# A short convolution moved from VectorE to TensorE: four diagonal tap matrices per channel block, accumulated in PSUM

## The chip, the cores and the metric

The kernel runs on one core of one Trainium2 chip. The metric is the device time of one execution in microseconds (us). In a profile PE is TensorE's matmul side and PEld its weight loads, DVE is VectorE, ACT is ScalarE, POOL is GpSimd, and SP is SyncE, which here only issues DMAs.

## What is computed

One block of a network with adaptive layer norm, on 16 sequences of 512 steps and 256 channels in float32: a modulated layer norm, a bidirectional Mamba (two directions, 512 inner channels, 64 states, a causal convolution of 4 taps per channel), a second norm, and a gated network with 1024 hidden units. The part that matters is, for each direction:

```python
xz = x @ W_in.T
xp, z = jnp.split(xz, 2, axis=-1)
xc = conv_general_dilated(xp.transpose(0, 2, 1), conv_w[:, None, :], window_strides=(1,),
                          padding=[(K - 1, 0)], feature_group_count=E)      # K = 4 taps, E = 512 channels
xc = _silu(xc.transpose(0, 2, 1) + conv_b)
x_dbl = xc @ W_xp.T                       # dt_lo, B, C
dt = softplus(dt_lo @ W_dt.T + dt_b)
h = exp(dt * A) * h + (dt * xt) * B       # a scan over 512 steps, for 512 channels x 64 states
y = sum_n(h * C)
```

## The kernel before, in words

**The loop.** The program handles one sequence per *body*: a preparation body ("pre"), then "first", 14 times "mid" (a hardware loop), "last" and "tail". A body with scans has 128 *units*, 64 for each direction. A unit is 4 states of 128 channels: a tile `state` of 128 partitions by 2048 elements, handled in two halves of 1024.

**The scan pipeline.** For each unit ACT makes the decays (L985, four activations), the input of the scan `driven` is made in PSUM, DVE scans it (L1196, one `TENSOR_TENSOR_SCAN` per half), POOL multiplies the result by C (L1226, one per half), and PE sums over states into `y_ps` (L824, `accumulate`). In even units DVE makes `driven` itself (L1185), from rows that PE spreads into `b_ps` (L800). In odd units ACT (L998) and POOL (L1234) make `v_sb`, and PE transposes it into `driven` (L810, `drive`). Two halves of `driven` exist, so that PE's transposes for half h of an odd unit wait for the scan of half h of the even unit before.

**The side work.** Everything else is put between the units by tables (`side_steps`), as (unit, part, name, count): in a unit each engine first does its share of the scan pipeline and then its side steps. Part "early" and "late" are the previous sequence's output and hidden network (PE bank `q_ps`), "p1" is the second direction of this sequence (steps from unit `P1_AT` = 12), "next" the first direction of the next sequence (from `NEXT_AT` = 80); p1, next and the eight transposes `UT0` to `UT7` of the scan's input share the bank `p_ps`. Each engine runs its instructions in the order written, and each step in a bank waits (`bank_free`) until the step before it in the same bank has been read out.

**The convolution.** In p1 and next, for each of four channel blocks m, three units apart: PE makes the projection X (two matmuls of 128x512, L681) into `p_ps`; ACT copies it to `u_sb`, the inner part of `u_pad` whose first three columns are zero (L889), and writes tap 0 plus the bias into `xc` (L892); DVE adds taps 1, 2 and 3 with three `scalar_tensor_tensor` (L1156, steps `conv{m}0` and `conv{m}1`). Then ACT applies silu to `xc` (L896), and PE makes B, C and dt from it. In a mid body the blocks of p1 start in units 14, 17, 20 and 23 and those of next in 82, 85, 88 and 91.

**Other work in the same units.** In p1's units 15 to 22 DVE has the residual mix and a layer norm of part early. In next's units PE has the hidden network's first layer (`F`, four matmuls of 128x256 in each of units 77 to 84) and second layer (`H`, four in each of units 89 to 104); DVE multiplies the gate (`glu`, L1139, units 86 and 87) once ACT's silu of unit 85 is done (L957).

**Queues.** SP issues all DMAs in order: in each unit `c_rep` (256 KB, L504, which waits for POOL's reading of two units before), and between them `ud_rep`, weights, stores. `dt_sb` (128 partitions by 8 KB) holds dt, is written in the steps D (L918) and stored to DRAM by `store_ud`; between this store and the next stage's D it is not used, except that C is staged in its first block.

## Time and profile before

| | |
|---|---|
| median of 3 runs | 14339.97 us (14336.53 to 14356.86) |
| the profiled execution | 14347.66 us |
| its span in the profile | 14345.8 us |
| first scan to the end | from 146.8 us on |
| TensorE clock granted, mean | 0.81 |

A row of the costliest groups reads: line, engine, operation, tile written <- tiles read, count | busy us in all, mean ns of one | idle us of the engine just before them, and who ended most of it. A row of a timeline reads: start us, duration us, engine, line, what, count of instructions merged, and in brackets the idle time before it. PE's fp32 matmuls stand in the trace as two records each, so that two matmuls of 128x512 read "x4".

### The profile page before, as it was taken

How to read it: one execution, taken by the hardware profiler on the slowest of the kernel's cores; microseconds unless marked ns; L12 is line 12 of the kernel's file. 1: busy time of each engine (PE TensorE's matmuls, PEld its weight loads, DVE VectorE, ACT ScalarE, POOL GpSimd, SP SyncE). 2: the span in 40 equal slices, each digit the busy share in tenths (PEclk: the TensorE clock that was granted, in tenths of full speed). 3: DMA queues.
4: the chain of work that ended last, by engine and by line, in shares of the span. 5: the costliest groups of instructions: out<-in, count | busy, mean ns of one | idle time of the engine just before them, and what ended most of it. 6: DMA issues, size and time to landing. Idle time of an engine off the chain costs nothing.

```text
span 14345.8 us, 177084 instructions
## 1 busy us (share of the span) xinstructions
PE 10529.0 (73%) x50188; PEld 6035.3 (42%) x50188; DVE 13278.1 (93%) x8254; ACT 10969.1 (76%) x23324; POOL 10908.2 (76%) x5124
## 2 busy tenths in 40 slices
PE   5567767777676777767777777776777767777776
PEld 2234434444343443434434344443444434344345
DVE  6999999999999999999999999999999999999992
ACT  5777777788777887778777777777777877787782
POOL 4887777787777777778777777777777777777781
PEclk7778878788787887878888788887878878788798
DMA  2223323333232332323322233232333323233232
GB/s 72 80 82 98 103 89 108 99 104 104 90 107 95 107 105 95 106 91 109 107 95 96 94 109 105 97 102 91 107 98 105 104 88 107 95 108 103 94 110 87
DMA packets 596164, 1414.30 MB, mean 99 GB/s; under 512 B 63488, under 2 KB 104592, under 8 KB 594976
## 3 DMA queue, kind: packets, MB, share of 16 engines
q1 hardware_dynamic: 595104, 1402.00, 29.9%
q8 instruction: 441, 7.23, 0.2%
q14 instruction: 619, 5.07, 0.1%
HBM read 1313.57 MB, written 88.18 MB: 98 GB/s over the span
## 4 chain that ended last, share of the span: by engine, by line
issue 26%; PE 26%; DVE 24%; ACT 20%; POOL 3%; DVEq 1%; DMA 0%; ACTq 0%; POOLq 0%; SPq 0%
DVE state L1196 13%; PE driven L810 7%; ACT state L985 7%; ACT v_sb L998 6%; PE q_ps L765 6%; DVE driven L1185 3%; POOL state L1226 3%; PE y_ps L824 3%; PE p_ps L681 2%; PE q_ps L752 2%; DVE xc L1156 2%; PE b_ps L800 2%; PE q_ps L775 1%; ACT L985 1%; PE p_ps L688 1%
## 5 line engine op out<-in xcount | busy, mean ns | idle before, releaser
L1226 POOL TENSOR_TENSOR state<-state,c_rep 128x1024 f32<-128x1024 f32 x4096 | 9764.5, 2406 | 3006.0 <-DVE state L1196 3005.4
L1196 DVE TENSOR_TENSOR_SCAN state<-state,driven 128x1024 f32<-128x1024 f32 x4096 | 9106.1, 2270 | 444.8 <-PE driven L810 274.1
L998 ACT ACTIVATE v_sb<-u_t,b_t 128x128 f32<-128x128 f32 x12288 | 3992.7, 505 | 2226.7 <-PE driven L810 2224.8
L985 ACT ACTIVATE state<-ud_rep,cols_sb 128x512 f32<-128x512 f32 x8192 | 5185.8, 710 | 2.4 <-PE y_ps L824 0.2
L824 PE MATMUL y_ps<-state,consts_sb 128*32 128x512 f32 x16384 | 2666.9, 729 | 2292.1 <-POOL state L1226 2289.1
L810 PE MATMUL driven<-consts_sb,v_sb 128*128 128x128 f32 x16384 | 2957.9, 344 | 1122.8 <-DVE state L1196 1113.4
L810 PEld LDWEIGHTS driven<-consts_sb,v_sb 128*128 128x128 f32 x16384 | 2432.5, 179 | 2576.9 <-DVE state L1196 2134.0
L1185 DVE TENSOR_TENSOR driven<-ud_rep,b_ps 128x1024 f32<-128x1024 f32 x2048 | 2390.2, 1213 | 16.9 <-DMA ud_rep<-ud_rows 16.9
L765 PE MATMUL q_ps<-hid,wq_sb 128*128 128x256 f32 x8192 | 2231.1, 420 | 130.0 <-ACT hid L963 83.4
L765 PEld LDWEIGHTS q_ps<-hid,wq_sb 128*128 128x128 f32 x8192 | 1596.9, 205 | 926.1 <-issue 671.7
L824 PEld LDWEIGHTS y_ps<-state,consts_sb 128*32 128x32 f32 x16384 | 347.5, 117 | 3418.0 <-POOL state L1226 3027.9
L1234 POOL TENSOR_TENSOR v_sb<-u_t,b_t 128x512 f32<-128x512 f32 x1024 | 1220.1, 1191 | 140.0 <-ACT u_t L913 140.0
L681 PE MATMUL p_ps<-x_t,wp_sb 128*128 128x512 f32 x1024 | 580.0, 695 | 20.7 <-ACT sz L936 14.5
L800 PE MATMUL b_ps<-b_parts,onehot 32*128 32x512 f32 x1024 | 587.1, 573 | 0.0
L752 PE MATMUL q_ps<-xn_q,wq_sb 128*128 128x256 f32 x2048 | 542.3, 410 | 44.3 <-ACT hid L953 39.9
L963 ACT ACTIVATE hid<-q_ps,cols_sb 128x256 f32<-128x256 f32 x512 | 239.0, 467 | 436.6 <-PE q_ps L765 436.2
L1156 DVE SCALAR_TENSOR_TENSOR xc<-u_pad,cols_sb,xc 128x512 f32<-128x512 f32 x384 | 510.5, 1329 | 51.6 <-ACT xc L892 40.5
L752 PEld LDWEIGHTS q_ps<-xn_q,wq_sb 128*128 128x128 f32 x2048 | 388.6, 200 | 243.0 <-issue 143.9
L775 PE MATMUL q_ps<-wq_sb,hid 128*128 128x256 f32 x1024 | 308.5, 454 | 37.1 <-ACT hid L968 30.1
L681 PEld LDWEIGHTS p_ps<-x_t,wp_sb 128*128 128x128 f32 x1024 | 208.8, 214 | 264.9 <-issue 212.9
L953 ACT ACTIVATE hid<-q_ps,cols_sb 128x256 f32<-128x256 f32 x512 | 212.6, 468 | 138.0 <-PE q_ps L752 137.7
L800 PEld LDWEIGHTS b_ps<-b_parts,onehot 32*128 32x128 f32 x1024 | 214.5, 209 | 227.0 <-issue 227.0
(113 smaller groups left out, 5202.5 us busy)
## 6 DMA issues: line engine op xcount, KB each, us to landing
c_rep<-bc_rows SPq DMA_DIRECT2D x2048, 256.0 KB, 3.0
ud_rep<-ud_rows SPq DMA_DIRECT2D x512, 512.0 KB, 3.9
wq_sb<-in_h SPq DMA_DIRECT2D x512, 512.0 KB, 3.8
wq_sb<-in_f SPq DMA_DIRECT2D x128, 512.0 KB, 4.4
wp_sb<-in_win SPq DMA_DIRECT2D x64, 512.0 KB, 3.8
ud_rows<-u_pad SPq DMA_DIRECT2D x128, 256.0 KB, 3.3
ud_rows<-dt_sb SPq DMA_DIRECT2D x128, 256.0 KB, 3.4
u_nat<-ud_rows SPq DMA_DIRECT2D x128, 256.0 KB, 3.1
```

The lines of the kernel that those rows point to most:

```text
L681: mm = pe.matmul(p_ps[:], wp_sb[:, m, k, :], x_t[:, k, :], start=(k == 0), stop=(k == DC - 1))
L752: mm = pe.matmul(q_ps[:, which * TH:(which + 1) * TH], w[:, m % 2, which, k, :], n_t[:, k, i * TH:(i + 1) * TH], start=(k == 0), stop=(k = ...
L765: mm = pe.matmul(q_ps[:, 0:TH], w[:, k, :], src[:, k, :], start=(k == 0), stop=(k == HC - 1))
L800: pe.matmul(b_ps[:], onehot[k, g % quarter, :], b_parts[d][k, :], start=True, stop=True).then_inc(b_spread, 1)
L810: mm = pe.transpose(driven[:, q % DRIVE_RING, j % 2, tt * P:(tt + 1) * P], v_sb[:, unit // 2 % V_RING, tt, j].rearrange("p e n -> p (e n)" ...
L824: mm = pe.matmul(y_ps[EG * j:EG * (j + 1), :], over_nn, state[:, k % STATE_RING, j, :], start=(g == 0), stop=(g == NG - 1))
L985: ins = act.activation(state[:, unit % STATE_RING, j, :], ud_rep[:, nth % 2, j, 1, :], ACT.Exp, scale=a_neg[:, d, c, j, g:g + 1])
L998: ins = act.activation(v_sb[:, unit // 2 % V_RING, tt, :, :, n].rearrange("p j e -> p (j e)"), u_t[:, nth % 2, tt, :], ACT.Identity, scale ...
L1185: dve.tensor_tensor(driven[:, h], u_rows(unit)[:, 2 * h:2 * h + 2], b_ps[:].unsqueeze(1).to_broadcast([P, 2, T]), ALU.mult).then_inc(dve_d ...
L1196: dve.tensor_tensor_scan(flat, flat, driven[:, q % DRIVE_RING].rearrange("p j t -> p (j t)"), 0.0, ALU.mult, ALU.add).then_inc(scanned, 1)
L1226: pool.tensor_tensor(part, part, c_rep[:, unit % ROW_RING, :].unsqueeze(1).to_broadcast([P, 2, T]), ALU.mult).then_inc(was_read, 1)
L1234: pool.tensor_tensor(v_sb[:, unit // 2 % V_RING, TT - 1].rearrange("p j e n -> p (j e) n"), u_t[:, nth % 2, TT - 1, :].unsqueeze(2).to_bro ...
```

## The change

The four taps of a channel block become four matmuls whose stationary matrix is the diagonal matrix of one tap (128x128) and whose moving operand is `u_pad` shifted by the tap's number of columns, all accumulated in `p_ps` (step `K{m}`, two matmuls in each of the two units after X). ACT then writes `xc` from `p_ps` with the bias in one activation; the activation for tap 0 and DVE's three instructions per block go. The matrices are made once at the start by ACT (32 activations of 128x128 into `ud_rep`), stored to a DRAM tensor of 2 MB, and loaded, 1 MB for each direction, into `dt_sb` (`load_conv`), in unit 8 for p1 and 76 for next. The transposes `UT2`, `UT6` and `UT7` move from units 25, 89 and 106 to 26, 78 and 97.

```diff
-UT_AT = (120, 10, 25, 41, 57, 73, 89, 106)
+UT_AT = (120, 10, 26, 41, 57, 73, 78, 97)
...
-        act.append((x, part, f"X{m}", 2))
-        dve += [(x + 1 + i, part, f"conv{m}{i}", 1 + i) for i in range(2)]
+        act.append((x, part, f"X{m}", 1))
+        pe += [(x + 1 + i, part, f"K{m}", i) for i in range(2)]
+        act.append((x + 2, part, f"K{m}", 1))
...
+        conv_dram = nc.dram_tensor("conv_taps", (2, P, EC * TAPS * P), F32, kind="Internal").ap()
...
+        conv_w = dt_sb[:].rearrange("p c t -> p (c t)").rearrange("p (c k n) -> p c k n", c=EC, k=TAPS)
...
+            sp.wait_ge(setup_act, 4)
+            sp.dma_start(conv_dram.rearrange("d p n -> p d n"),
+                         conv_made.rearrange("p d c k n -> p d (c k n)")).then_inc(conv_stored, 16)
             sp.wait_ge(mod_stored, 16)
+            sp.wait_ge(conv_stored, 16)
...
+            def load_conv(at, part):
+
+                if at.kind != "pre":
+                    wait(ud_out.sem, ud_out.before(at) if part == "p1" else ud_out.done(at, "p1", "ud"))
+                d = 1 if part == "p1" else 0
+                sp.dma_start(dt_sb[:].rearrange("p c t -> p (c t)"), conv_dram[d]).then_inc(conv_in.sem, 16)
...
+                    if unit == P1_AT - 4 and at.has("p1"):
+                        load_conv(at, "p1")
+                    if unit == NEXT_AT - 4 and at.has("next"):
+                        load_conv(at, "next")
...
+                elif name[0] == "K":
+                    m = int(name[1])
+                    if quarter == 0:
+                        pe.wait_ge(act_side.sem, act_side.done(at, part, f"X{m}"))
+                        if m == 0:
+                            pe.wait_ge(conv_in.sem, conv_in.done(at, part, "conv"))
+                    for k in range(2 * quarter, 2 * quarter + 2):
+                        mm = pe.matmul(p_ps[:], conv_w[:, m, k, :], u_pad[:, m, k:k + T], start=(k == 0), stop=(k == TAPS - 1))
...
+            for d in range(2):
+                for c in range(EC):
+                    for k in range(TAPS):
+                        ins = act.activation(conv_made[:, d, c, k, :], ident, ACT.Identity, scale=taps[:, d, c, k:k + 1])
+            ins.then_inc(setup_act, 1)
...
-                        act.wait_ge(done, act_side.done(at, part, name, 0))
-                        act.activation(xc_sb[d][:, m, :], u_pad[:, m, 0:T], ACT.Identity, bias=conv_b[:, d, m:m + 1],
-                                       scale=taps[:, d, m, 0:1]).then_inc(done, 1)
+                    elif kind == "K":
+                        after_pe(pe_p)
+                        act.activation(xc_sb[d][:, m, :], p_ps[:], ACT.Identity, bias=conv_b[:, d, m:m + 1]).then_inc(done, 1)
                     elif name == "xc":
-                        act.wait_ge(dve_side.sem, dve_side.done(at, part, "conv31"))
+                        act.wait_ge(done, act_side.done(at, part, "K3"))
...
-                    if name.startswith("conv"):
-                        m, last = int(name[4]), int(name[5])
-                        if not last:
-                            dve.wait_ge(act_side.sem, act_side.done(at, part, f"X{m}"))
-                        dst = xc_sb[d][:, m, :]
-                        for i in ((2, 3) if last else (1,)):
-                            emit(dve.scalar_tensor_tensor(dst, u_pad[:, m, i:i + T], taps[:, d, m, i:i + 1], dst,
-                                                          ALU.mult, ALU.add), i < TAPS - 1)
```

**Order on PE, units 91 to 93 of a mid body (part next).** Before, from the transposes for unit 93 on; `q_ps` is the hidden network, `y_ps` the sum over states:

```order
L810 MATMUL driven<-consts_sb,v_sb 128x128 x16
L797 REGISTER_ALU
L800 MATMUL b_ps<-b_parts,onehot 128x512
L765 MATMUL q_ps<-hid,wq_sb 128x256 x4
L822 REGISTER_ALU
L824 MATMUL y_ps<-state,consts_sb 32x512 x4
L650 REGISTER_ALU
L762 REGISTER_ALU
L765 MATMUL q_ps<-hid,wq_sb 128x256 x4
```

The same place with the change, where the four matmuls of block 3's taps stand in units 92 and 93:

```order
L840 MATMUL driven<-consts_sb,v_sb 128x128 x16
L827 REGISTER_ALU
L830 MATMUL b_ps<-b_parts,onehot 128x512
L795 MATMUL q_ps<-hid,wq_sb 128x256 x4
L672 REGISTER_ALU
L711 MATMUL p_ps<-u_pad,dt_sb 128x512 x2
L852 REGISTER_ALU
L854 MATMUL y_ps<-state,consts_sb 32x512 x4
L672 REGISTER_ALU
L792 REGISTER_ALU
L795 MATMUL q_ps<-hid,wq_sb 128x256 x4
L711 MATMUL p_ps<-u_pad,dt_sb 128x512 x2
```

Each of the two units now has a second side step on PE, between the transposes and the next sums.

**Order on ACT, units 84 and 85 of a mid body.** Before, from the first part of `v_sb` in unit 84 to the silu (L957) of the hidden network:

```order
L998 ACTIVATE v_sb<-u_t,b_t 128x128 x4
L866 REGISTER_ALU
L953 ACTIVATE hid<-q_ps,cols_sb 128x256 x2
L998 ACTIVATE v_sb<-u_t,b_t 128x128 x8
L985 ACTIVATE state<-ud_rep,cols_sb 128x512 x4
L956 REGISTER_ALU
L957 ACT_TABLE_LOAD
L957 ACTIVATE hid<-hid 128x2048
```

With the change:

```order
L1033 ACTIVATE v_sb<-u_t,b_t 128x128 x4
L901 REGISTER_ALU
L988 ACTIVATE hid<-q_ps,cols_sb 128x256 x2
L901 REGISTER_ALU
L928 ACTIVATE xc<-p_ps,cols_sb 128x512
L1033 ACTIVATE v_sb<-u_t,b_t 128x128 x8
L1020 ACTIVATE state<-ud_rep,cols_sb 128x512 x4
L991 REGISTER_ALU
L992 ACT_TABLE_LOAD
L992 ACTIVATE hid<-hid 128x2048
```

The read-out of block 0's taps now stands in unit 84 ahead of the decays and the silu, and waits for PE's second pair of tap matmuls.

## Rows read from the trace of the kernel before

**Rows 1.** The profile's page, part 1: busy time of each engine over the span.
```profile
PE 10529.0 (73%) x50188; PEld 6035.3 (42%) x50188; DVE 13278.1 (93%) x8254; ACT 10969.1 (76%) x23324; POOL 10908.2 (76%) x5124
```
**Rows 2.** The page, part 5: costliest groups.
```profile
L1196 DVE TENSOR_TENSOR_SCAN state<-state,driven 128x1024 f32<-128x1024 f32 x4096 | 9106.1, 2270 | 444.8 <-PE driven L810 274.1
...
L998 ACT ACTIVATE v_sb<-u_t,b_t 128x128 f32<-128x128 f32 x12288 | 3992.7, 505 | 2226.7 <-PE driven L810 2224.8
...
L681 PE MATMUL p_ps<-x_t,wp_sb 128*128 128x512 f32 x1024 | 580.0, 695 | 20.7 <-ACT sz L936 14.5
...
L1156 DVE SCALAR_TENSOR_TENSOR xc<-u_pad,cols_sb,xc 128x512 f32<-128x512 f32 x384 | 510.5, 1329 | 51.6 <-ACT xc L892 40.5
```
**Rows 3.** Timeline of DVE, units 78 to 80, where it has no side step.
```profile
3260.49 8.81 DVE L1196 TENSOR_TENSOR_SCAN state<-state,driven 128x1024 f32<-128x1024 f32 x4
3269.22 2.33 DVE L1185 TENSOR_TENSOR driven<-ud_rep,b_ps 128x1024 f32<-128x1024 f32 x2
3271.46 4.46 DVE L1196 TENSOR_TENSOR_SCAN state<-state,driven 128x1024 f32<-128x1024 f32 x2
```
**Rows 4.** Windows of one body's two convolution stretches, line L1156 alone: DVE busy, clock, DMA.
```profile
2816.00:2916.00 100.00, 15.60 (x12) 0.67 0.18 56
3283.00:3373.00 90.00, 16.42 (x12) 0.82 0.28 95
```
**Rows 5.** The view of line L1156: durations in ns, min/median/max.
```profile
L1156 DVE SCALAR_TENSOR_TENSOR xc<-u_pad,cols_sb,xc x384: 736/962/2808, 61.0 to 13441.3; 128x512 f32<-128x512 f32 x192
```
**Rows 6.** Waits of DVE in that body (2722 to 3599): total, times, longest, in us.
```profile
DVE state L1196 <- PE driven L810: 17.4, 13, 4.2
...
DVE xc L1156 <- ACT xc L892: 1.5, 2, 1.2
DVE state L1196 <- DVE xc L1156: 1.2, 4, 0.6
```
**Rows 7.** Timeline of PE, units 100 to 102: two side steps in each unit.
```profile
3416.47 1.97 PE L810 MATMUL driven<-consts_sb,v_sb 128*128 128x128 f32 x16
...
3418.80 1.99 PE L765 MATMUL q_ps<-hid,wq_sb 128*128 128x256 f32 x8
3420.63 1.89 PE L697 MATMUL p_ps<-sz,xc 128*128 128x64 f32 x16
...
3428.10 1.97 PE L810 MATMUL driven<-consts_sb,v_sb 128*128 128x128 f32 x16
```
**Rows 8.** Timeline of PE, units 88 to 91: a wait, and two projections X.
```profile
3333.09 1.97 PE L810 MATMUL driven<-consts_sb,v_sb 128*128 128x128 f32 x8 [2.80 <-DVE state L1196]
...
3337.89 3.65 PE L681 MATMUL p_ps<-x_t,wp_sb 128*128 128x512 f32 x4
...
3354.81 1.88 PE L681 MATMUL p_ps<-x_t,wp_sb 128*128 128x512 f32 x4
```
**Rows 9.** Timelines of ACT, units 84 and 85, and of DVE at the gate, unit 86.
```profile
3303.28 1.42 ACT L998 ACTIVATE v_sb<-u_t,b_t 128x128 f32<-128x128 f32 x4 [0.62 <-PE driven L810]
...
3314.47 1.91 ACT L957 ACTIVATE hid<-hid 128x2048 f32<-128x2048 f32 x1
...
3316.41 3.19 DVE L1139 TENSOR_TENSOR hid<-hid 128x1024 f32<-128x1024 f32 x1 [0.55 <-ACT hid L957]
```
**Rows 10.** Timeline of the start: the exp ahead, SP's load of x, blocks 0 and 2 of X.
```profile
12.88 0.63 ACT L854 ACTIVATE cols_sb<-cols_sb 128x512 f32<-128x512 f32 x1
...
27.11 0.38 SPq L551 DMA_DIRECT2D xa<-in_x  x1
...
55.19 3.75 PE L681 MATMUL p_ps<-x_t,wp_sb 128*128 128x512 f32 x4 [0.78 <-ACT x_t L879]
...
65.80 1.98 PE L681 MATMUL p_ps<-x_t,wp_sb 128*128 128x512 f32 x4 [1.54 <-ACT xc L892]
```
**Rows 11.** DMA issues: count, KB each, median us from issue to landing.
```profile
c_rep<-bc_rows SPq DMA_DIRECT2D x2048, 256.0 KB, 3.0
...
state<-in_wmod SPq DMA_DIRECT2D x1, 1536.0 KB, 7.2
```

More of the change, by code:

```diff
@@ L286, in adaln_kernel @@
         w3s = at_setup[0:BATCH, 13 * T:13 * T + D]
+        conv_made = ud_rep[:, 0].rearrange("p j s t -> p (j s t)").rearrange("p (d c k n) -> p d c k n", d=2, c=EC, k=TAPS)
         driven = ctx.enter_context(nc.psum_tensor("driven", [P, DRIVE_RING, 2, T], F32))
@@ L314, in adaln_kernel @@
         out_stored = Signal(sem("out_stored"), [(0, "late", "out", 1)], 16)
+        conv_in = Signal(sem("conv_in"), [(0, "p1", "conv", 1), (1, "next", "conv", 1)], 16)
+        conv_stored = sem("conv_stored")
         wp_in = Signal(sem("wp_in"), [(0, "p1", "w0", 1), (1, "p1", "w1", 1), (2, "o0", "wout", 1), (3, "next", "w0", 1),
@@ L466, in load_wdt @@
                 d = 1 if part == "p1" else 0
-                wait(dve_side.sem, dve_side.done(at, part, "conv31"))
+                wait(act_side.sem, act_side.done(at, part, "X3"))
                 sp.dma_start(wdt_sb[d], wdt[:, d, :]).then_inc(wdt_in.sem, 16)
+            def load_conv(at, part):
[3 more added lines that the diff above has]
+                sp.dma_start(dt_sb[:].rearrange("p c t -> p (c t)"), conv_dram[d]).then_inc(conv_in.sem, 16)
             def load_wxp(at, part):
@@ L920, in step @@
                         act.wait_ge(done, act_side.done(at, part, "D3"))
-                        act.wait_ge(dve_side.sem, dve_side.done(at, part, "conv31"))
+                        act.wait_ge(pe_p.sem, pe_p.done(at, part, "K3"))
                         act.activation(u_sb, dt_sb[:], ACT.Abs).then_inc(done, 1)
@@ L1149, in step @@
                     d = 1 if part == "p1" else 0
-                    if name.startswith("conv"):
-                        m, last = int(name[4]), int(name[5])
-                        if not last:
-                            dve.wait_ge(act_side.sem, act_side.done(at, part, f"X{m}"))
-                        dst = xc_sb[d][:, m, :]
-                        for i in ((2, 3) if last else (1,)):
-                            emit(dve.scalar_tensor_tensor(dst, u_pad[:, m, i:i + T], taps[:, d, m, i:i + 1], dst,
-                                                          ALU.mult, ALU.add), i < TAPS - 1)
-                    elif name == "BC":
+                    if name == "BC":
                         dve.wait_ge(act_side.sem, act_side.done(at, part, name))
```

## The prediction

> **What bounds the kernel now.** The page's busy line comes first: DVE is busy for 93% of the span, the others for 73 to 76% [rows 1]. So I ask where DVE's time goes. The costliest groups give most of it to the scans, and 510.5 us to the 384 convolution instructions, with 51.6 us of idle time before them [rows 2]. The timeline of DVE then shows the pace without side work: four scans and two products make a pair of units, 3271.46 - 3260.49 = 10.97 us, and DVE never stands [rows 3]. Every DVE instruction in a unit therefore lengthens the body, unless something else is as late. Last come the others' limits. PE's timeline with two side steps in each of two units runs without a gap from 3416.47 to 3428.10, 11.63 us for the pair; one side step takes 3420.63 - 3418.80 = 1.83 us, so the pipeline alone takes 11.63 - 4 x 1.83 = 4.3 us [rows 7]. Three side steps fit under DVE's 10.97 us (9.8 us), four do not. This holds at the clock's upper level, 2.4 GHz. At the lower, 1.2 GHz, PE needs twice as long: a projection X takes 3.65 us there and 1.88 us here [rows 8].
>
> **What the change removes.** In one mid body the convolution holds DVE for 15.60 us in p1 and 16.42 us in next [rows 4]. With it go its waits for ACT, 1.5 us (all in next), and the scans' waits for its last write, 1.2 us [rows 6], of which I give 0.8 to p1. That is 16.4 us per p1 stage and 18.3 us per next stage. There are 16 p1 stages and 15 next stages inside the scans (one more lies in the preparation): 262 + 275 = **537 us** on the bounding engine. One instruction takes 1329 ns on average; its shortest takes 736 ns and its longest 2808 ns [rows 5]. The range of prices for one is thus 0.74 to 1.33 us; I take the mean, since the scans queue behind the whole of it. The Trainium skill (SBUF - State Buffer, "SBUF: two separate sides") says that a DVE operation with two SBUF inputs and a GpSimd operation exclude each other by a lock on a shared port; the long ones here would be such waits. Someone who priced only DVE's own work would expect 384 x 0.74 = 284 us; by the rule as by the row, the wait also goes.
>
> **What it adds on PE.** Each block gets four matmuls of 128x512, as two side steps of two. The projections X are the same shape: two take 1.88 us at the upper and 3.65 us at the lower level [rows 8]; all 512 of X and Z took 580.0 us [rows 2], and K adds 512 more, so about 580 us on an engine that has 3800 us free [rows 1]. The Trainium skill (FP8 and Floating Point Precision, "TensorE Precision Notes") gives four passes for true FP32, an estimate of 4 x 512 / 2.4 GHz = 0.85 us each; the row has 0.94 us. What it costs depends on the pair of units:
> - p1 (units 14 to 25): two side steps per pair, at most four in 24 and 25, two of them transposes of some 1 us. 4.3 + 4 x 1.83 us is not reached; hidden at the upper level, also behind DVE's norm and mix.
> - next: units 82/83 (F, X; F, K), 90/91 (H, K; H, X) and 92/93 (H, K; H, K) have four. Each gives back 11.63 - 10.97 = 0.66 us: **2.0 us**. The pairs 84/85 and 88/89 have three and are hidden.
> - The lower clock. PE falls to it where it stands: after a wait of 2.80 us the transposes of unit 89 take 1.97 us and X takes 3.65 us [rows 8]. (The windows show 0.67 and 0.82 of the full clock in the two stretches [rows 4].) Where such a spell meets four side steps, DVE waits for PE, up to 4.2 us [rows 6]; 3.5 us of that is the clock's part (4.2 - 0.66). Until now the convolution on DVE covered such spells. I charge one newly bare spell per stage, **3.5 us** each; from below it is 0 (a denser PE stays up, as in units 100 to 102), from above three per stage.
>
> **What it adds elsewhere.** ACT's number of activations per block stays at two, of the same shape. But in unit 84 the read-out of K stands ahead of the silu: from the end of the transposes ACT needs 1.4 us for `v_sb`, then waits until PE has spread, F and K behind it (0.4 + 2 x 1.83 = 4.1 us), 0.6 us to read, 2.6 and 2.5 us for the next `v_sb` and decays, 1.3 + 1.9 us for the table and silu: 13.0 us, near the 3316.38 - 3303.28 = 13.1 us of today [rows 9]. DVE comes earlier, though: after the transposes' last slot it has a scan pair, two products and a scan pair, 4.46 + 2.33 + 4.46 = 11.2 us [rows 3], less the 1.1 us of the transposes themselves. The gate's wait grows from 0.55 us to about 3: **2.5 us** per next stage. UT2, now in unit 26, stands ahead of ACT's silu of `xc` and of the decays behind it: its read-out costs **0.6 us** per p1 stage. UT6 and UT7 in units 78 and 97 fall where PE has 4.3 + 2 x 1.83 + 0.6 and 4.3 + 3 x 1.83 + 0.6 us, 10.4 us at most, under 10.97: nothing. UT7 makes PE wait for DVE's product of BC in unit 97 ahead of the next sums, but DVE's next scan still has 2.2 us to go by then.
>
> SP loads 1 MB twice per body. From 7.2 us for 1536 KB [rows 11], I estimate 4.8 us of the queues each. The `c_rep` issued just before goes first; the next follows a unit later, after 4.4 us or more, so it is hardly touched: nothing, and rival 2 if not.
>
> **The start.** The 32 activations cost ACT 32 x 3992.7 / 12288 = 10.4 us [rows 2], from 13.5 us [rows 10] to 24 us, beside DVE's set-up. The 2 MB store is an estimated 9.6 us (7.2 x 2048 / 1536) and starts at about 25 us, so the load of x at 27.11 us [rows 10] comes 7.5 us later. The preparation runs X and K by turns with nothing beside: K's four matmuls take 2 x 3.75 us in the first block and 2 x 1.98 us in three more [rows 10], 19 us, less some 3.5 us for DVE's and ACT's waits that go: 15.5. Together **+23 us**.
>
> **The sum.** p1: 16 x (16.4 - 3.5 - 0.6) = 197 us. next: 15 x (18.3 - 2.0 - 3.5 - 2.5) = 155 us. Less 23: 329 us off the profiled execution's 14347.7 us, 14018.7. The runs' median lies 7.7 us under that execution: I forecast **14,010 us**, 2.3% less.
>
> **Rivals.**
> 1. *Everything is covered.* PE's extra work lifts its clock and ACT's lateness is absorbed by the four-deep ring of states: only the start costs. 14,340 - 537 + 23 = 13,826 us. For it: PE stayed at the upper level through units 100 to 102, its densest. Against: ACT's silu and the four-step pairs are plain arithmetic. 13%.
> 2. *The loads hold up POOL.* If the 1 MB stands ahead of a `c_rep` that lands in 3.0 us today [rows 11], POOL waits up to 4 us, and then PE and DVE. 31 loads x 4 = 124 us: 14,134 us; with a second bare clock spell per stage (31 x 3.5 = 108) 14,240 us. Against: the order of issue above. 14%.
> 3. *Slower: TensorE stays at 1.2 GHz in the convolution stretches.* They already have a granted clock of 0.67 and 0.82 [rows 4], that is, two thirds and a third of their time at the lower level. next's six pairs hold 3 x 11.63 + 2 x 9.8 + 8.0 = 62.5 us of PE work; at 3.65 / 1.88 it is 121 us against 90 - 18.3 = 72 us of DVE's, 49 us of waiting against 18.3 saved, 15 x 31 = 465 us. p1 (five pairs of 8.0 and one of 10: 50 us of work, 97 against 100 - 16.4 = 84) gains 16 x 3 = 48 us still; with the start near 14,780 us if all is low. It turns slower than before once about three quarters of PE's time in both stretches is low. Against: PE falls after standing, and K fills that standing; PE at the lower level and always busy has nowhere been seen to last. The Trainium skill (TensorE: Matmul & The Clock Gate, "HAM oscillation") warns of exactly this: idle gaps send a matmul stream back to half rate. The trace agrees: after the wait eight transposes take 1.97 us, as long as sixteen in units 100 to 102 [rows 7, 8]. 11%.
> 4. *The waits eat it all*, no change (within 0.2%, 29 us, about what a measurement here can tell): 4%. DVE's convolution instructions are gone from the order, so the change does do what it says.
>
> **How the numbers follow.** 58% is for the forecast. Its own range is 13,900 (no bare spell: 31 x 3.5 = 108 us less) to 14,120 (two). Rival 1 below and most of rival 2 above make the 80% range 13,850 to 14,200 us. Faster: 58 + 13 + 14 = 85%; same 4%; slower 11%.
>
> **What would show it.** DVE busy falls by about 510 us to some 12,770, PE busy rises by about 580; in the page's groups no DVE line writes `xc` from `u_pad`. In units 90 to 93 DVE waits for `driven` by about 0.7 us a pair, at unit 86 for ACT's silu by about 3 us, and POOL waits for no DMA. The mean clock rises from 0.81. It is wrong if DVE's waits for `driven` (274 us in all, [rows 2]) more than double, if matmuls of L711 mostly take twice 1.88 us a pair, or if `c_rep` ends POOL's waits.

## The result and the profile after

The changed kernel takes **13,807.6 us** (median of 4 runs, 13,802.35 to 13,812.14) against 14,338.25 us for the kernel before beside it: a ratio of 0.9627 (95% interval 0.9611 to 0.9644), 3.7% faster. The forecast was 14,010 us with a range down to 13,850: the direction was right, the gain about 200 us too small, and the time lies below the range. Rival 1 (everything is covered, 13,826 us, given 13%) comes within 19 us. One execution in the whole record, a sixth of e2 below, took 16,514 us at a granted clock of 0.55 and is left out.

The page of the changed kernel, parts 1, 2, 5 and 6 (columns as before):

```profile
PE 10525.1 (76%) x51212; PEld 5964.6 (43%) x51212; DVE 12755.6 (92%) x7870; ACT 10903.7 (79%) x23356; POOL 10839.3 (79%) x5124
...
PEclk7778888888898888888888888887888889888898
...
L1223 DVE TENSOR_TENSOR_SCAN state<-state,driven 128x1024 f32<-128x1024 f32 x4096 | 9104.2, 2271 | 405.1 <-PE driven L840 255.3
L1033 ACT ACTIVATE v_sb<-u_t,b_t 128x128 f32<-128x128 f32 x12288 | 3980.4, 504 | 1814.7 <-PE driven L840 1811.2
...
L711 PE MATMUL p_ps<-u_pad,dt_sb 128*128 128x512 f32 x1024 | 555.3, 669 | 26.7 <-ACT u_pad L924 25.6
...
L703 PE MATMUL p_ps<-x_t,wp_sb 128*128 128x512 f32 x1024 | 524.2, 636 | 18.4 <-ACT sz L971 14.5
...
c_rep<-bc_rows SPq DMA_DIRECT2D x2048, 256.0 KB, 3.0
...
dt_sb<-conv_taps SPq DMA_DIRECT2D x32, 1024.0 KB, 5.2
```

Against [rows 1, 2, 11]: DVE's busy time fell by 13,278.1 - 12,755.6 = 522.5 us, as foreseen. The scans' idle time fell from 444.8 to 405.1 us and the part that waits for `driven` from 274.1 to 255.3 us, where I had expected it to rise. That fall is the sum of three movements that the experiments below take apart: 205.2 us with nothing but the transposes moved (e1), 240.9 with the convolution gone from DVE as well (e9), 255.3 with the taps on PE. The tap matmuls (L711) hold PE for 555.3 us, near the 580 I took, and yet PE's total is 10,525.1 against 10,529.0 us: the mean granted clock rose from 0.81 to 0.856, and most other groups of matmuls got cheaper, X and Z (now L703) from 580.0 to 524.2 us. Not all of this is the taps' doing: without any tap PE's total is 10,246.5 us (e9), so that the taps add 279 us to it, half of the time that they hold PE. `c_rep` still lands in 3.0 us in the median.

The same three windows of one mid body in both kernels: units 14 to 25 (p1), 82 to 95 (next), and the whole body. The columns are the time, the busy time of PE, PEld, DVE, ACT and POOL with instruction counts, the granted clock, DMA share and GB/s. Before:

```profile
4569.42:4670.10 100.68, 58.58 (x242) 27.36 (x242) 98.63 (x71) 62.97 (x139) 67.27 (x31) 0.67 0.17 55
5037.67:5138.49 100.82, 70.95 (x337) 40.06 (x336) 98.00 (x58) 75.27 (x159) 74.71 (x36) 0.81 0.27 91
4476.35:5353.63 877.28, 648.97 (x3136) 372.43 (x3136) 831.57 (x516) 685.85 (x1459) 681.00 (x320) 0.82 0.31 101
```

After:

```profile
4399.44:4484.15 84.71, 63.84 (x259) 29.82 (x260) 83.38 (x59) 57.78 (x131) 64.19 (x31) 0.80 0.20 65
4853.09:4940.28 87.19, 78.67 (x366) 41.70 (x364) 79.94 (x45) 74.55 (x158) 73.21 (x36) 0.92 0.31 105
4306.34:5149.11 842.77, 654.80 (x3202) 370.76 (x3200) 798.01 (x491) 681.32 (x1458) 677.65 (x320) 0.86 0.33 107
```

In p1 16.0 us go and PE's clock rises from 0.67 to 0.80; in next 13.6 us go and it rises from 0.81 to 0.92. PE does 64 matmul records more per body, worth 64 x 555.3 / 1024 = 35 us, and is busy for only 6 us more than before, or 17.5 us more than in the body without taps (637.34 us, e9).

**Where the 539 us of span went** (from the starts of the first scans of units, in both traces): the first scan comes at 159.5 us instead of 146.8 (+12.7); the first body takes 780.3 instead of 820.8 us (-40.5); the 14 mid bodies 11,788.5 instead of 12,282.8 us (-494.3); the last one to its last unit 780.6 instead of 796.8 us (-16.2). Within a mid body (medians over the 14, in us; the columns of four experiments are used below):

| units | before | after | only the transposes moved (e1) | no convolution (e9) | `UT6`, `UT7` back (e5) | `glu` later (e7) |
|---|---|---|---|---|---|---|
| 14 to 25 (p1) | 100.71 | 84.71 | 100.71 | 84.71 | 84.70 | 84.70 |
| 26 to 29 | 25.23 | 26.48 | 28.09 | 26.00 | 26.47 | 26.48 |
| 82 to 95 (next) | 100.77 | 87.20 | 100.80 | 84.14 | 89.96 | 83.76 |
| of these, 86/87 | 19.34 | 16.26 | 19.34 | 17.18 | 16.26 | 13.77 |
| of these, 88/89 | 13.32 | 10.97 | 13.32 | 10.97 | 10.97 | 12.42 |
| of these, 90/91 | 14.67 | 13.80 | 14.68 | 12.09 | 16.55 | 10.97 |
| 96 to 99 | 24.82 | 23.80 | 24.84 | 24.22 | 23.80 | 23.81 |
| 100/101 | 15.28 | 12.02 | 12.02 | 12.02 | 12.02 | 12.01 |
| 102 to 127 | 175.05 | 173.03 | 173.10 | 173.20 | 173.64 | 173.10 |
| 96 to 127 together | 215.12 | 208.85 | 209.96 | 209.44 | 209.46 | 208.92 |
| body | 877.23 | 842.92 | 873.85 | 839.72 | 846.07 | 839.63 |

**What the forecast foresaw in next.** DVE's timeline in units 84 to 93 after the change:

```profile
4869.45 4.46 DVE L1223 TENSOR_TENSOR_SCAN state<-state,driven 128x1024 f32<-128x1024 f32 x2 [0.93 <-PE driven L840]
...
4883.12 1.23 DVE L1174 TENSOR_TENSOR hid<-hid 128x1024 f32<-128x1024 f32 x1 [2.59 <-ACT hid L992]
...
4910.48 4.46 DVE L1223 TENSOR_TENSOR_SCAN state<-state,driven 128x1024 f32<-128x1024 f32 x2 [2.72 <-PE driven L840]
...
4922.06 4.46 DVE L1223 TENSOR_TENSOR_SCAN state<-state,driven 128x1024 f32<-128x1024 f32 x2 [0.50 <-PE driven L840]
```

The gate waits 2.59 us for ACT's silu, against 0.55 before [rows 9], but its product behind the wait then takes 1.23 us where it took 3.19. Over all bodies unit 86 has a wait of 2.59 us (median) and a product of 1.25 us (mean), against 0.61 and 3.08 before: together 3.84 for 3.69 us, so that DVE loses next to nothing at the gate. The four side steps of PE in units 90 and 91 give back 0.50 us in unit 93, since PE's transposes for an odd unit stand behind the side steps of the two units before it; those of 82 and 83 give back the 0.93 us in unit 85. And one bare spell of the lower clock is there (PE is slow in it and DVE waits for PE), 2.72 us in unit 91, behind the three side steps of units 88 and 89. PE's timeline ahead of it:

```profile
4883.72 3.65 PE L711 MATMUL p_ps<-u_pad,dt_sb 128*128 128x512 f32 x4 [1.62 <-ACT u_pad L924]
...
4894.66 1.97 PE L840 MATMUL driven<-consts_sb,v_sb 128*128 128x128 f32 x8 [2.21 <-DVE state L1223]
4896.84 1.97 PE L840 MATMUL driven<-consts_sb,v_sb 128*128 128x128 f32 x8 [0.21 <-DVE state L1223]
...
4899.46 3.78 PE L703 MATMUL p_ps<-x_t,wp_sb 128*128 128x512 f32 x4
...
4906.54 1.88 PE L711 MATMUL p_ps<-u_pad,dt_sb 128*128 128x512 f32 x4
```

After a wait of 2.21 us eight transposes take 1.97 us and X 3.78 us, the lower level, 1.2 GHz (granted clock 0.50); 7 us later two tap matmuls take 1.88 us, the upper level (1.00). The Trainium skill (TensorE: Matmul & The Clock Gate, "HAM oscillation") says that idle gaps send a stream of matmuls back to half rate. The trace agrees as to this fall; the consequence that rival 3 drew from it did not come.

### The profile page after: what moved, and what is told of

Same layout as the page of the kernel before. It is cut to its first block, busy times and chain, and to the rows that moved or that the text cites. A ratio compares the mean times of both kernels' runs of the same rounds, so it can differ in the third digit from the quotient of the medians.

```text
span 13806.5 us, 178788 instructions
## 1 busy us (share of the span) xinstructions
PE 10525.1 (76%) x51212; PEld 5964.6 (43%) x51212; DVE 12755.6 (92%) x7870; ACT 10903.7 (79%) x23356; POOL 10839.3 (79%) x5124
## 4 chain that ended last, share of the span: by engine, by line
PE 28%; issue 25%; ACT 22%; DVE 20%; POOL 4%; DVEq 1%; DMA 0%; ACTq 0%; SPq 0%; POOLq 0%
DVE state L1223 11%; ACT state L1020 7%; ACT v_sb L1033 7%; PE driven L840 7%; PE q_ps L795 6%; PE y_ps L854 4%; POOL state L1253 3%; DVE driven L1212 3%; PE q_ps L782 2%; PE p_ps L703 2%; PE b_ps L830 2%; PE p_ps L711 1%; ACT L1020 1%; PE q_ps L805 1%; PE p_ps L727 1%
## 5 line engine op out<-in xcount | busy, mean ns | idle before, releaser
L1223 DVE TENSOR_TENSOR_SCAN state<-state,driven 128x1024 f32<-128x1024 f32 x4096 | 9104.2, 2271 | 405.1 <-PE driven L840 255.3
L1020 ACT ACTIVATE state<-ud_rep,cols_sb 128x512 f32<-128x512 f32 x8192 | 5175.3, 708 | 2.2
L854 PE MATMUL y_ps<-state,consts_sb 128*32 128x512 f32 x16384 | 2541.8, 693 | 1878.3 <-POOL state L1253 1875.9
L840 PE MATMUL driven<-consts_sb,v_sb 128*128 128x128 f32 x16384 | 2768.7, 328 | 968.6 <-DVE state L1223 958.6
L840 PEld LDWEIGHTS driven<-consts_sb,v_sb 128*128 128x128 f32 x16384 | 2273.2, 170 | 2308.9 <-DVE state L1223 1881.7
L795 PE MATMUL q_ps<-hid,wq_sb 128*128 128x256 f32 x8192 | 2142.5, 407 | 125.4 <-ACT hid L998 77.1
L795 PEld LDWEIGHTS q_ps<-hid,wq_sb 128*128 128x128 f32 x8192 | 1541.8, 198 | 878.9 <-issue 641.7
L1261 POOL TENSOR_TENSOR v_sb<-u_t,b_t 128x512 f32<-128x512 f32 x1024 | 1178.0, 1150 | 152.0 <-ACT u_t L948 152.0
L711 PE MATMUL p_ps<-u_pad,dt_sb 128*128 128x512 f32 x1024 | 555.3, 669 | 26.7 <-ACT u_pad L924 25.6
L703 PE MATMUL p_ps<-x_t,wp_sb 128*128 128x512 f32 x1024 | 524.2, 636 | 18.4 <-ACT sz L971 14.5
L998 ACT ACTIVATE hid<-q_ps,cols_sb 128x256 f32<-128x256 f32 x512 | 237.2, 463 | 356.8 <-PE q_ps L795 356.7
L711 PEld LDWEIGHTS p_ps<-u_pad,dt_sb 128*128 128x128 f32 x1024 | 196.9, 206 | 258.7 <-issue 203.0
L703 PEld LDWEIGHTS p_ps<-x_t,wp_sb 128*128 128x128 f32 x1024 | 194.1, 199 | 229.7 <-issue 150.5
```

The lines of the kernel that those rows point to most:

```text
L703: mm = pe.matmul(p_ps[:], wp_sb[:, m, k, :], x_t[:, k, :], start=(k == 0), stop=(k == DC - 1))
L795: mm = pe.matmul(q_ps[:, 0:TH], w[:, k, :], src[:, k, :], start=(k == 0), stop=(k == HC - 1))
L840: mm = pe.transpose(driven[:, q % DRIVE_RING, j % 2, tt * P:(tt + 1) * P], v_sb[:, unit // 2 % V_RING, tt, j].rearrange("p e n -> p (e n)" ...
L854: mm = pe.matmul(y_ps[EG * j:EG * (j + 1), :], over_nn, state[:, k % STATE_RING, j, :], start=(g == 0), stop=(g == NG - 1))
L1020: ins = act.activation(state[:, unit % STATE_RING, j, :], ud_rep[:, nth % 2, j, 1, :], ACT.Exp, scale=a_neg[:, d, c, j, g:g + 1])
L1223: dve.tensor_tensor_scan(flat, flat, driven[:, q % DRIVE_RING].rearrange("p j t -> p (j t)"), 0.0, ALU.mult, ALU.add).then_inc(scanned, 1)
```

## The experiments

Two questions: is PE's added work free, and does it lift the clock? And which part of the edit removed the wait of unit 101, which the forecast had left alone? The kernel before ran beside each and took 14,338.8 to 14,340.0 us, against 14,338.25 us beside the changed kernel, so times of different experiments can be compared to within 2 us.

### e1: only the transposes moved

Against the kernel before:

```diff
-UT_AT = (120, 10, 25, 41, 57, 73, 89, 106)
+UT_AT = (120, 10, 26, 41, 57, 73, 78, 97)
```

> The kernel before with nothing but the three transposes UT2, UT6 and UT7 moved to units 26, 78 and 97. Theory A (the added tap matmuls lift TensorE's clock and so end the waits of DVE in units 100 to 120): time within 30 us of 14,338, mean clock 0.81, the wait of about 4 us at unit 101 stays. Theory B (moving the transposes ended these waits): 14,338 - 16 x 5.4 = about 14,250 us, the wait at unit 101 falls under 1.5 us, with the clock nearly unchanged.

Measured: 14,294.6 us (14,286.8 to 14,296.0), ratio 0.9968 (0.9957 to 0.9980), clock 0.811. The new places of `UT2`, `UT6` and `UT7` are worth 44 us by themselves: theory B by the place and by the clock, at half of the size that I gave it (some 88 us). The table shows where: 3.3 us per body in the pair 100/101 and 2.0 in units 102 to 127 (units 30 to 81 give another 1.1), less 2.9 in units 26 to 29, where `UT2`'s read-out now makes ACT's decays late. Before, DVE at unit 101 and PE ahead of it:

```profile
5171.97 4.46 DVE L1196 TENSOR_TENSOR_SCAN state<-state,driven 128x1024 f32<-128x1024 f32 x2 [4.21 <-PE driven L810]
```

```profile
5156.85 1.72 PE L810 MATMUL driven<-consts_sb,v_sb 128*128 128x128 f32 x8 [1.09 <-DVE state L1196]
...
5159.22 3.78 PE L765 MATMUL q_ps<-hid,wq_sb 128*128 128x256 f32 x8
```

and DVE at the same scan in e1:

```profile
5153.72 4.46 DVE L1196 TENSOR_TENSOR_SCAN state<-state,driven 128x1024 f32<-128x1024 f32 x2 [0.94 <-PE driven L810]
```

Before, the spell at the lower clock (`H` 3.78 us where 1.99 is the upper level's) fell on units 98 to 100, where each unit has two side steps. In e1 it does not, without a single tap matmul in the program. PE's waits for DVE ahead of unit 99 are 0.47 and 1.09 us there, with UT7's transposes now in unit 97, where they were 1.40 and 1.09 us before. The three moves were made together, and which of them does it was not run. I had [rows 6] with its longest wait of 4.2 us, and used it as the price of a bare spell; I had not asked whether the change removes that very wait.

### e2: the tap matmuls beside the convolution

DVE's convolution stays. PE does the 512 matmuls as well, with the identity as the stationary matrix; nothing reads what they write, and the step behind them in the bank waits for no read-out. Against e1:

```diff
+        pe += [(x + 1 + i, part, f"K{m}", i) for i in range(2)]
...
+                elif name[0] == "K":
+                    m = int(name[1])
+                    for k in range(2 * quarter, 2 * quarter + 2):
+                        mm = pe.matmul(p_ps[:], ident, u_pad[:, m, k:k + T], start=(k == 0), stop=(k == TAPS - 1))
```

> The kernel before with the moved transposes, plus the 512 matmuls of 128x512 in the places of the taps (identity as stationary operand, results never read), while DVE still does the convolution. Theory A: the work costs PE's busy line far less than 580 us, since the clock rises (0.85 or more); the time does not grow, and falls by the 3 to 5 us per body of the waits in units 100 to 120: 14,250 to 14,340 us. Rival (work is work, as the prediction charged it): PE busy up by 500 us or more, clock 0.82 or lower, time 14,400 us or more.

Measured: 14,285.3 us (median of five, 14,277.3 to 14,296.1), ratio 0.9963 (0.9950 to 0.9977). Its page, and its windows of units 14 to 25, 82 to 95 and of the body:

```profile
PE 10728.9 (75%) x51212; PEld 6092.2 (43%) x51212; DVE 13271.2 (93%) x8254; ACT 10930.5 (77%) x23324; POOL 10921.0 (76%) x5124
```

```profile
4555.35:4656.12 100.77, 72.19 (x270) 33.87 (x270) 98.72 (x72) 62.92 (x138) 67.38 (x31) 0.75 0.18 55
5027.07:5126.91 99.84, 80.01 (x366) 42.51 (x364) 97.60 (x58) 75.12 (x158) 75.19 (x36) 0.91 0.26 91
4462.28:5336.43 874.15, 664.32 (x3200) 378.44 (x3200) 830.27 (x515) 683.58 (x1458) 683.75 (x320) 0.85 0.31 101
```

PE's busy time grows by 303 us over e1's 10,425.9. The added matmuls hold it for 556.8 us, so the others take 254 us less. The clock rises from 0.811 to 0.842, a little under the 0.85 that I had expected, and the time does not grow (14,294.6 in e1). So under DVE's old pace the matmuls are free, and nearly half of their work is paid back by the clock that they raise.

### e9: no convolution on either engine

e1 with a convolution that costs nothing but tap 0 on ACT:

```diff
-        dve += [(x + 1 + i, part, f"conv{m}{i}", 1 + i) for i in range(2)]
...
-                        act.wait_ge(dve_side.sem, dve_side.done(at, part, "conv31"))
+                        act.wait_ge(done, act_side.done(at, part, "X3"))
```

> The kernel before with moved transposes and without DVE's three convolution instructions per block; no tap matmuls either (taps 1 to 3 of the convolution are left out). Theory A (each us of DVE is a us of the body while its spells of low clock are covered by nothing else): 14,295 - 15.5 x 35 = about 13,750 us. On the clock: if the tap matmuls lift it, it stays at 0.82 or lower here against 0.842 with one tap and 0.856 with four; if the shorter waits of PE for DVE lift it, it comes to 0.84 or more without them. The prediction's fear (spells of low clock laid bare once DVE's convolution is gone): DVE's waits for driven grow by 7 us per body, time 13,850 us or more.

Measured: 13,760.7 us (13,758.4 to 13,770.0), ratio 0.9597 (0.9581 to 0.9613), clock 0.828, first scan at 138.6 us. Its whole body, and the groups of waits of its DVE (total, times, longest):

```profile
4283.78:5123.31 839.53, 637.34 (x3136) 366.21 (x3136) 798.16 (x491) 682.69 (x1458) 678.82 (x320) 0.83 0.32 105
```

```profile
DVE state L1195 <- PE driven L809: 240.9, 261, 2.9
...
DVE hid L1138 <- ACT hid L956: 107.0, 17, 34.1
```

Five readings. First, taking DVE's convolution out is worth 873.85 - 839.72 = 34.1 us per body over e1; the forecast had 16.4 + 18.3 = 34.7. Second, the changed kernel's body is 842.92 us: four taps on PE, 32 matmuls or 32 x 0.94 = 30 us of PE work, cost 3.2 us, 3.1 of it in units 82 to 95; p1 takes 84.71 us in both. (The two also differ in ACT's order: here it writes `xc` right behind X, there two units later. The 3.2 us hold that as well.) Third, the gate's longer wait is not the tap read-out's doing: e9 has it too (107.0 us in all, 103.5 in the changed kernel, 76.5 before). DVE simply comes earlier to the same silu. Fourth, on the clock the run lies between my two cases: it goes from 0.811 to 0.828 without a tap in the program, so the quicker pace alone lifts it a little, and the taps bring the rest up to 0.856. Fifth, the fear of bare spells did not come true: DVE's waits for `driven` grow from 205.2 us in e1 to 240.9, some 2.3 us per body and not 7.

### e10: one of DVE's three instructions

e1 with tap 1 alone on DVE, beside tap 0 on ACT:

```diff
-        dve += [(x + 1 + i, part, f"conv{m}{i}", 1 + i) for i in range(2)]
+        dve.append((x + 1, part, f"conv{m}0", 1))
```

> The same with one of DVE's three convolution instructions per block kept (taps 2 and 3 are left out). Theory A: between the two in proportion to DVE's busy time on the line, no step: about two thirds of 545 us of gain, 13,900 to 13,960 us. Rival (the gain comes from the dependency ACT, DVE, ACT going, not from DVE's busy time): most of the gain only at zero instructions, 14,100 us or more.

Measured: 13,972.9 us (13,967.5 to 13,984.3), ratio 0.9742 (0.9726 to 0.9759), clock 0.831. With three instructions per block the time is 14,294.6, with one 13,972.9, with none 13,760.7 us: the first costs 212 us for 128 instructions (1.66 us each), the next two 322 us for 256 (1.26 us each). The time lies 13 us above my range, and far below the rival's 14,100. All three cost 534 us, 1.39 us each, beside 510.5 + 51.6 = 562 us of busy time and waits in [rows 2]; 0.74 us, the shortest in [rows 5], would give 284. The price of DVE work here is thus close to its whole time in the trace, with waits, and the mean of 1.33 us was the right one of the two ends.

### e3 and e4: one tap matmul, and eight

From the changed kernel: e3 does tap 3 alone, e4 each tap twice. First e3, then e4:

```diff
-                    for k in range(2 * quarter, 2 * quarter + 2):
-                        mm = pe.matmul(p_ps[:], conv_w[:, m, k, :], u_pad[:, m, k:k + T], start=(k == 0), stop=(k == TAPS - 1))
+                    mm = None
+                    if quarter:
+                        mm = pe.matmul(p_ps[:], conv_w[:, m, 3, :], u_pad[:, m, 3:3 + T], start=True, stop=True)
```

```diff
-                    for k in range(2 * quarter, 2 * quarter + 2):
+                    for k in range(4 * quarter, 4 * quarter + 4):
+                        k = k % TAPS
```

> The changed kernel with one tap matmul per block instead of four (the convolution is left out but for the last tap); DVE stays relieved. Theory A: clock falls back to 0.81 to 0.83 and PE busy falls by less than the 416 us of the 384 matmuls left out; the four-step pairs in units 84 to 95 give back about 4.6 us per body, a low-clock wait at unit 101 returns with about 3.3 us: 13,770 to 13,800 us. Rival (work alone counts): 4.6 us x 15 and nothing lost, 13,740 us or less, clock as in the changed kernel, 0.856.

> The changed kernel with every tap matmul done twice (the first round is overwritten). Theory A with PE at its upper level: PE's steps exceed DVE's 10.97 us by 2.5 us more in units 82/83, 3.7 us in 92/93, 2.7 us in 24/25 and some tenths elsewhere, 8 to 10 us per body: 13,940 to 13,970 us, clock 0.88 or more, PE busy up by some 450 us. Rival (low clock): clock at or under 0.856, PE busy up by 600 us or more, time over 14,050 us.

| tap matmuls per block | time, us | ratio (95%) | clock | PE busy | first scan | body | units 14 to 25 | 82 to 95 |
|---|---|---|---|---|---|---|---|---|
| 0 (e9) | 13,760.7 | 0.9597 (0.9581, 0.9613) | 0.828 | 10,246.5 | 138.6 | 839.72 | 84.71 | 84.14 |
| 1 (e3) | 13,743.1 | 0.9583 (0.9567, 0.9599) | 0.842 | 10,244.9 | 153.2 | 838.85 | 84.71 | 82.19 |
| 4 (the change) | 13,807.6 | 0.9627 (0.9611, 0.9644) | 0.856 | 10,525.1 | 159.5 | 842.92 | 84.71 | 87.20 |
| 8 (e4) | 13,941.8 | 0.9723 (0.9707, 0.9740) | 0.863 | 10,854.5 | 177.3 | 849.87 | 85.22 | 94.00 |

One tap is as fast as none, and in next 2 us faster: it costs PE no busy time at all (10,244.9 against 10,246.5 us), and the clock is higher. ACT's order differs between e9 and e3, as said above; e2, which adds nothing but matmuls to e1, has next 1.0 us shorter too. From four to eight PE has hardly any slack left in next: the granted clock there is 0.98 in the window of units 82 to 95, and 6.8 us are lost in each such stage, where 16 more matmuls are 15 us of work. Even then p1 gives back only 0.5 us. My expectation for e3 was missed on the fast side, its clock of 0.842 lies above my 0.81 to 0.83, and the wait of unit 101 did not return there. The time of e4 came out as expected; its clock did not, which stopped at 0.863, and PE's busy time grew by 329 us where I had some 450.

### e5: the change with two transposes in their old places

```diff
-UT_AT = (120, 10, 26, 41, 57, 73, 78, 97)
+UT_AT = (120, 10, 26, 41, 57, 73, 89, 106)
```

> The changed kernel with UT6 and UT7 back in units 89 and 106 (UT2 stays in 26). If the moved transposes ended the wait at unit 101 here too, as they did beside the old convolution: that wait comes back with about 3.3 us, the pair 124/125 with up to 1.5: 13,808 + 15 x 3 to 5 = 13,850 to 13,885 us, clock within 0.01 of 0.856. If the tap matmuls' clock suffices: within 15 us of 13,808.

Measured: 13,855.4 us (13,843.8 to 13,863.1), ratio 0.9657 (0.9641 to 0.9673). The move is worth 48 us beside the taps, much as the 44 us without them, but at another place: the pair 100/101 stays at 12.02 us, and 90/91 goes from 13.80 to 16.55. That the time falls into my range for a wait that returns is luck, since that wait did not. DVE and PE in those units, in one of the two bodies where the pair takes 18.2 us:

```profile
4930.04 4.46 DVE L1223 TENSOR_TENSOR_SCAN state<-state,driven 128x1024 f32<-128x1024 f32 x2 [7.12 <-PE driven L840]
```

```profile
4921.20 0.60 PE L742 MATMUL p_ps<-consts_sb,u_nat 128*128 128x128 f32 x4
4924.36 2.91 PE L711 MATMUL p_ps<-u_pad,dt_sb 128*128 128x512 f32 x4 [2.57 <-ACT u_t L980]
```

`UT6` shares the bank `p_ps` with the taps: the tap matmuls wait 2.57 us until ACT has read the transposes out, and then take 2.91 us, at a granted clock of 0.66. Units 96 to 127 keep nearly all of their gain without the two moves: 215.1 us before, 209.5 here, 208.9 in the changed kernel. So the table of transposes is a part of the gain of this change, 9% of it, and without it the conv's own gain would be 14,339.2 - 13,855.4 = 484 us with `UT2` moved.

### e6, e7, e8: what DVE now waits for

Two waits of the changed kernel have other work ready behind them. e6 puts the softplus chain from `rest` on, Z and the stores behind it one unit later (DVE waited 6.4 us for ACT's `sz` near unit 108); e7 puts the two halves of the gate one unit later, into units 87 and 88; e8 does both. e6's edit of the changed kernel, without the stores and Z:

```diff
-    dve.append((s + 17, part, "rest", 1))
-    act.append((s + 18, part, "ln", 1))
+    dve.append((s + 18, part, "rest", 1))
+    act.append((s + 19, part, "ln", 1))
```

and e7's:

```diff
-        dve += [(f_at + HC + 1 + j, part, f"glu{i}{j}", 1) for j in range(2)]
+        dve += [(f_at + HC + 1 + i + j, part, f"glu{i}{j}", 1) for j in range(2)]
```

> The changed kernel with DVE's step rest and all steps behind it in the softplus chain one unit later, in p1 and next. Theory: the largest single waits left are of DVE for ACT's chain, 6.4 us at unit 108 and 2.5 at unit 40, in the shadow of nothing; a unit later they are covered: 13,808 - 15 x 6.4 - 16 x 2.5 = 13,672 us at best, 13,670 to 13,740 expected. Rival (ACT as a whole is the bound there, so the wait moves along): within 30 us of 13,808.

> The changed kernel with the two gate products of part late in units 87 and 88 instead of 86 and 87. Theory: the 2.6 us wait of DVE for ACT's silu at unit 86 goes, 15 x 2.6 = 39 us: 13,765 to 13,785 us. Rival (the second half of the hidden layer's input is then late for PE in unit 89): the time within 15 us of 13,808, with PE waiting for DVE's product in unit 89.

> Both edits of timing steps together (softplus chain from rest on, and the gate products, one unit later). If the two waits lie apart, the gains add: 13,640 to 13,700 us. If they share ACT's lateness: about what the softplus edit alone gives.

Measured: e6 13,740.5 us (ratio 0.9582, 0.9565 to 0.9598), e7 13,768.2 us (0.9597, 0.9581 to 0.9613), e8 **13,683.3 us** (13,671.4 to 13,697.9; 0.9543, 0.9527 to 0.9559). Against 13,807.6 us they gain 67, 39 and 124 us: the two together give at least their sum of 107, and e8 beats both kernels. e6 gives half of the 136 us that I had at best: DVE's wait for `sz` falls from 160.2 to 29.5 us in all, but its waits for ACT's decays (L1020) grow from 74.1 to 132.0, so a part of the wait moves along. e7 answers a question of the forecast. DVE and PE of e7 at the same place as shown above:

```profile
4879.71 2.88 DVE L1174 TENSOR_TENSOR hid<-hid 128x1024 f32<-128x1024 f32 x1
...
4900.24 4.46 DVE L1223 TENSOR_TENSOR_SCAN state<-state,driven 128x1024 f32<-128x1024 f32 x2 [0.84 <-PE driven L840]
```

```profile
4884.85 1.09 PE L840 MATMUL driven<-consts_sb,v_sb 128*128 128x128 f32 x8 [0.97 <-DVE state L1223]
4887.03 1.97 PE L840 MATMUL driven<-consts_sb,v_sb 128*128 128x128 f32 x8 [1.08 <-DVE state L1223]
4888.93 0.79 PE L830 MATMUL b_ps<-b_parts,onehot 32*128 32x512 f32 x1
4889.65 3.78 PE L703 MATMUL p_ps<-x_t,wp_sb 128*128 128x512 f32 x4
```

With DVE no longer waiting at the gate, PE's longest wait ahead of unit 89 is 1.08 us instead of 2.21, the fall of the clock comes eight transposes later, and the wait in unit 91 is 0.84 instead of 2.72 us; in eight of the 14 mid bodies the pair 90/91 takes 10.97 us, with no wait at all. The spell itself is still there (X takes 3.78 us), but it is hardly bare any more. At the gate little is won: the wait is gone, but the first product takes 2.8 us again instead of 1.25. In this one run the bare spell thus goes with the gate's wait, and the 87.20 - 83.76 = 3.4 us of units 82 to 95 are mostly the spell's.

## Why the prediction was wrong

**Right.** What bounds the kernel (DVE), what is removed and its price: 34.7 us per body, 34.1 by e9, and the choice of the mean over the shortest instruction (e10). The four-step pairs: 0.66 us each in three pairs; the trace has 0.93, 0.50 and 0.50 us in units 85, 93 and 95, behind the side steps of 82/83, 90/91 and 92/93. The wait at the gate: 2.5 us more, measured 2.59 - 0.55 = 2.0. The loads at nothing: `c_rep` 3.0 us, and the idle time of POOL's multiply is all DVE's; rival 2 is out. PE's 580 us of added matmuls: 555.3. Rival 3 is out: no stretch stays at the lower clock, p1's rose to 0.80.

**Wrong: "I charge one newly bare spell per stage, 3.5 us each".** That was 7.0 us per body, and the runs have 2.8. In p1 no spell is bare: units 14 to 25 take 84.71 us with no tap, with one and with four. PE does fall to the lower clock there, in the changed kernel too:

```profile
4416.67 1.97 PE L840 MATMUL driven<-consts_sb,v_sb 128*128 128x128 f32 x8 [2.34 <-DVE state L1223]
...
4421.46 3.78 PE L711 MATMUL p_ps<-u_pad,dt_sb 128*128 128x512 f32 x4
```

But DVE, busy for 83.38 of the 84.71 us with the norm and the mix of part early, never waits for PE in these units. The forecast had this cover in its line on p1 ("also behind DVE's norm and mix") and left it out of the charge for the clock. In next there is one bare spell, 2.72 us in unit 91 (the pair 90/91 takes 13.80 - 10.97 = 2.8 us too long), behind three side steps, so that all of it is the clock's; its bareness goes with the gate's wait (e7). The price came from the worst wait of the body [rows 6], and e1 shows that this very wait is one that the edit removes. That is 7.0 - 2.8 = 4.2 of the 11.7 us per body by which the forecast fell short.

**Wrong: "UT6 and UT7 ...: nothing".** I asked what the transposes cost at their new places, and took the waits that stand today in units 96 to 127 as staying. These units gain 6.3 us per body, 3.3 of it in the pair 100/101. This is the larger half of the error. e1 has 5.2 us of it by the moves alone; but e5, with `UT6` and `UT7` back and the convolution on PE, has 5.7 us of it too. Either edit thus ends most of these waits, and no run has neither of the two moves and neither convolution, so what ends them in e5 stays open. In the changed kernel the moves are worth their 48 us mostly elsewhere, 2.8 us per body in units 82 to 95. `UT2` was undersized the other way: 1.25 us in units 26 to 29 instead of 0.6.

**Wrong: the gate at "2.5 us".** The wait is near that size, but the product behind it got 1.8 us shorter in unit 86 (3.08 to 1.25 us), which the forecast left out: wait and product together cost 3.84 - 3.69 = 0.15 us more. That is another 2.3 us per body. No run was aimed at why the product is shorter; it is 2.8 us again where it does not wait (e7).

**The start: +23 predicted, +12.7 measured.** SP's load of x and the first blocks in the changed kernel:

```profile
13.29 9.44 ACT L888 ACTIVATE ud_rep<-consts_sb,cols_sb 128x128 f32<-128x128 f32 x32
...
32.26 0.38 SPq L569 DMA_DIRECT2D xa<-in_x  x1
...
64.85 3.67 PE L711 MATMUL p_ps<-u_pad,dt_sb 128*128 128x512 f32 x8 [0.73 <-ACT u_pad L924]
69.30 1.98 PE L703 MATMUL p_ps<-x_t,wp_sb 128*128 128x512 f32 x4 [0.78 <-ACT xc L928]
```

The load of x comes 32.26 - 27.11 = 5.2 us later, not 7.5 (10.4 us taken for the 32 activations, 9.44 measured). The four matmuls of the first block take 3.67 us, the upper level, where I had put the lower, 7.5. And what goes was undersized: e9 has its first scan 8.2 us earlier than before (1.7 of it from an earlier load of x; e1, whose convolution is as before, is 2.5 us earlier already), where I had credited 3.5 us.

**The sum.** Per mid body, against the forecast of -22.6 us and -34.3 measured: p1 with units 26 to 29 -14.75 for -12.3; next -13.6 for -10.3; units 96 to 127 -6.3 for 0; the rest +0.3 for 0. The mid bodies' mean differs by 35.3 us, 1.0 more than these medians. The first body gained 6.2 us more than a median one (40.5); no run was aimed at that, and it stays open. So does why the spells of the lower clock fall where they fall: the runs show that they move with PE's waits (e1, e5, e7), not by what rule.

**The chances.** Rival 1's mechanism, "PE's extra work lifts its clock", is what e2 shows, and it deserved more than 13%. Its number was good partly by luck: it charged 23 us for the start, nothing for the taps (3.2 us per body over e9), and credited nothing for the transposes.

## What to carry to other kernels

When work moves to an engine that stands a quarter of its time and has a clock that falls when it stands, price it first at what its neighbour rows say and then ask how much of that it pays back: here the first 128 of the added matmuls cost no time that the runs show, and 512 cost 3 us a body. For every step that an edit moves, look at both ends, the place it goes to and the one it leaves: in e1 units 100 to 127 gained 5.2 us a body, and the new place of `UT2` cost 2.9. A wait that serves as a price for new waits has to be one that the change leaves standing. A slow spell of another engine costs only where the bounding engine has nothing else to do, and when that engine comes earlier to a wait, read the instruction behind the wait too. Two waits of one chain, a few units apart, are to be tested as one cause before they are added.

## What the runs showed of the hardware

- With DVE's work unchanged, 512 added fp32 matmuls of 128x512 that hold PE for 556.8 us raised its busy time by 303 us (e2 over e1); with DVE's convolution gone, 555.3 us of them raised it by 279 us (the change over e9). With one matmul per block in place of none PE's busy time is the same within 2 us (e3, e9).
- The granted clock did not reach 1.0 as a mean: 0.828, 0.842, 0.856 and 0.863 with 0 (e9), 1, 4 and 8 tap matmuls per block; 0.811 with DVE's convolution in place and no taps (e1), 0.842 with four beside it (e2). In the window of units 82 to 95 it does come near with eight, 0.98.
- A load of 1024 KB lands in 5.2 us (median of 32); the 2048 loads of 256 KB stay at 3.0 us in the median, and POOL's multiply waits for none of them.
- DVE's first gate product (L1174, before L1139) takes 3.08 us in the mean in unit 86 before, 1.25 us after a longer wait in the changed kernel, and 2.83 us without a wait in e7. Why is not shown.
